# An attention and MLP layer on one core: the rotary halves share partitions, and the scores run as pairs of 64-row matmuls later in the stage

## The reference

```python
xn = layernorm(x)
q, k, v, g = xn @ Wq.T, xn @ Wk.T, xn @ Wv.T, xn @ Wg.T      # 16 heads of 128
q, k = rope(q), rope(k)            # [x1*cos - x2*sin, x2*cos + x1*sin]
s = clip(xn @ Ws1.T @ Ws2.T + bs2, -32, 32)                  # 64 slots a head
es, enz = exp(s), exp(-cumlogsumexp(s))                      # along the tokens
A = tril(q @ k.T * DK ** -0.5)
qv = softmax(enz * (A @ es))
o = tril((qv * enz) @ es.T) @ v
attn = (rmsnorm(o) * g_norm_weight * silu(g)) @ Wo.T
ffn = (gelu(xn @ Wgate.T) * (xn @ Wup.T)) @ Wdown.T          # 4-bit codes with scales
out = x + attn + ffn
```

## Time and profile before

| what | value |
|---|---|
| median of 3 runs | 1186.56 us (1185.05 to 3839.03) |
| profiled execution, its own time | 1186.13 us |
| its span, first to last instruction | 1184.4 us |
| PE, busy share | 94% |
| DVE, busy share | 80% |
| ACT, busy share | 54% |
| POOL, busy share | 35% |
| granted PE clock, mean | 0.986 |

### The profile page before, as it was taken

One profiled execution on the slowest core, in us unless ns is written; L12 is line 12 of the kernel. 1 busy time (PEld: TensorE's weight loads), 2 busy tenths in 40 slices (PEclk: granted clock), 3 DMA queues, 4 the chain that ended last, 5 costly groups with the idle time before them and its releaser, 6 DMA issues.

```text
span 1184.4 us, 20879 instructions
## 1 busy us (share of the span) xinstructions
PE 1114.7 (94%) x6872; PEld 941.6 (79%) x6872; DVE 943.1 (80%) x1808; ACT 642.1 (54%) x1748; POOL 419.6 (35%) x306
## 2 busy tenths in 40 slices
PE   6789999999999998999989999899998999999995
PEld 5568888888788887888878888788887888788884
DVE  6888887888868887888877888778886888877763
ACT  5355564655645565555655556464563565655451
POOL 5233242433513335232443324343251433523231
PEclk9899999999999999999999999999999999999998
DMA  4001000100001000010000100001000100000001
GB/s 157 1 1 74 1 1 1 52 22 1 1 2 73 1 1 2 1 73 1 1 3 1 74 1 1 3 16 59 1 1 2 73 1 1 1 2 19 1 19 36
DMA packets 9117, 23.19 MB, mean 20 GB/s; under 512 B 816, under 2 KB 5808, under 8 KB 7984
## 3 DMA queue, kind: packets, MB, share of 16 engines
q1 hardware_dynamic: 9008, 21.76, 5.0%
HBM read 19.66 MB, written 2.10 MB: 18 GB/s over the span
## 4 chain that ended last, share of the span: by engine, by line
PE 71%; issue 8%; DVE 6%; ACT 6%; POOL 3%; POOLq 0%; DVEq 0%; ACTq 0%
PE bank L203 17%; PE bank L205 16%; PE bank L204 16%; PE bank L292 5%; ACT xs L568 3%; PE bank L305 3%; PE bank L349 2%; DVE xs L860 2%; POOL qkT L1087 2%; PE bank L294 2%; DVE Wt L740 2%; ACT xs L567 2%; PE bank L282 1%; PE bank L338 1%; PE bank L341 1%
## 5 line engine op out<-in xcount | busy, mean ns | idle before, releaser
L1096 POOL TENSOR_TENSOR inter_lo<-ffb,inter_hi 128x512 fp32r<-128x512 f32 x64 | 83.3, 1323 | 433.2 <-ACT inter_hi L617 433.2
L1087 POOL TENSOR_TENSOR qkT<-ra,xs 128x512 f32<-128x512 f32 x128 | 163.5, 1277 | 95.1 <-DVE xs L860 67.6
L586 ACT ACTIVATE sm<-bank,mx 128x64 f32<-128x64 f32 x256 | 76.3, 325 | 168.5 <-DVE mx L816 168.5
L857 DVE TENSOR_TENSOR ra<-bank,rope 128x512 f32<-128x512 f32 x128 | 88.0, 687 | 55.1 <-ACT xs L568 54.9
L805 DVE RECIPROCAL enzT<-enzT 128x256 f32<-128x256 f32 x64 | 111.6, 1744 | 0.0
L860 DVE TENSOR_TENSOR xs<-xs,rope 128x512 f32<-128x512 f32 x128 | 109.0, 852 | 0.0
L203 PE MATMUL bank<-xh,wqk_hi 128*128 128x512 f32 x256 | 107.4, 420 | 0.0
L203 PE MATMUL bank<-xh,wgu_hi 128*128 128x512 f32 x256 | 106.9, 418 | 0.0
L591 ACT ACTIVATE At<-bank 128x128 f32<-128x128 f32 x128 | 35.4, 276 | 132.0 <-DVE At L740 132.0
L205 PE MATMUL bank<-xh,wgu_lo 128*128 128x512 f32 x256 | 101.6, 397 | 0.0
L203 PE MATMUL bank<-wvg_hi,xh 128*128 128x512 f32 x256 | 101.4, 396 | 0.0
(11 more groups left out here) (137 smaller groups left out, 3211.5 us busy)
## 6 DMA issues: line engine op xcount, KB each, us to landing
raw<-in_w_qkvg SPq DMA_DIRECT2D x8, 1024.0 KB, 4.9
scaled<-in_w_scaled SPq DMA_DIRECT2D x8, 640.0 KB, 7.7
packed<-in_w_packed SPq DMA_DIRECT2D x8, 384.0 KB, 5.4
acc<-in_x SPq DMA_DIRECT2D x4, 512.0 KB, 8.6
out<-acc SPq DMA_DIRECT2D x4, 512.0 KB, 3.0
ws_raw<-in_w_slot SPq DMA_DIRECT2D x8, 48.0 KB, 1.8
rope<-in_rope_tab SPq DMA_DIRECT2D x1, 256.0 KB, 7.0
osq<-in_w_slot SPq DMA_DIRECT2D x1, 128.0 KB, 3.3
```

The source lines that it names most:

```text
L857: dve.tensor_tensor(two(ra[i % 2][:, :]), two(pj[i][:, :]), cos, ALU.mult).then_inc(cos_done, 1)
L1087: pool.tensor_tensor(qkT[:, i, :], ra[i % 2][:, :], xs[i % 2][:, :], ALU.add).then_inc(roped, 1)
L1096: pool.tensor_tensor(inter[1][e][:, :], ffb[e][:, :], inter[0][e][:, :].bitcast(F32), ALU.subtract).then_inc(inter_lo, 1)
```

## The change

Five edits belong together. The weights are laid out on the host so that a projection tile holds the same half of both heads: tile 0 has the first half of q of head 0 on partitions 0 to 63 and of head 1 on 64 to 127, tile 1 their second halves, tiles 2 and 3 the same for k. With this both operands of the rotation stand on the same partitions, `swap_halves` is gone from ACT, DVE makes eight products a stage straight from PSUM, and POOL subtracts or adds. The scores contract over 64 rows twice, as pairs of the two heads. The `sc` banks no longer alternate from stage to stage. On PE the scores move behind MLP tiles 1 and 2, `slot_weights` of sequence 1 moves ahead of q and k projection 3, the `es` transposes move ahead of `slot_weights` of sequence 0, and v and gate projection 2 moves behind `slot_rows`.

```diff
@@ PE
-                pe.wait_ge(cos_done, 4 * st + i + 1)
+                pe.wait_ge(rope_mul, 8 * st + 4 * (i // 2) + 3 + i % 2)
...
-            def scores(st, bp, i, hp):
-                h, b = i // 2, i % 2
-                if b == 0:
-                    pe.wait_ge(roped, 4 * st + 2 * h + 2)
-                dst = sc_bank(bp, "A", i)
+            def scores(st, b):
                 t0 = b * T
-                pe.matmul(dst[:, 0:T], qkT[:, 2 * h + 1, t0:t0 + P], qkT[:, 2 * h, t0:t0 + T],
-                          start=True, stop=True)
-                pe.matmul(dst[:, T:T + P], qkT[:, 2 * h + 1, t0 + P:t0 + T], qkT[:, 2 * h, t0 + P:t0 + T],
-                          start=True, stop=True).then_inc(A_full, 1)
+                pair = [(sc[h], slice(h * HALF, (h + 1) * HALF)) for h in range(2)]
+                for half in range(2):
+                    for dst, g in pair:
+                        pe.matmul(dst[:, 0:T], qkT[g, 2 + half, t0:t0 + P], qkT[g, half, t0:t0 + T],
+                                  start=half == 0, stop=half == 1)
+                for half in range(2):
+                    for dst, g in pair:
+                        mm = pe.matmul(dst[:, T:T + P], qkT[g, 2 + half, t0 + P:t0 + T],
+                                       qkT[g, half, t0 + P:t0 + T], start=half == 0, stop=half == 1)
+                mm.then_inc(A_full, 2)
...
-                for i in (0, 1):
...
-                    scores(st, bp, i, hp)
                 mlp_up(st, bp, hp, 0)
                 mlp_up(st, bp, hp, 1)
-                for i in (2, 3):
-                    pe.wait_ge(A_off, 4 * st + i - 1)
-                    scores(st, bp, i, hp)
+                pe.wait_ge(roped, 4 * st + 4)
+                if first:
+                    pe.wait_ge(J_ready, 1)
+                    pe.wait_ge(clip_done, 1)
+                else:
+                    pe.wait_ge(W_off, 4 * st)
+                scores(st, 0)
                 mlp_up(st, bp, hp, 2)
+                pe.wait_ge(A_off, 4 * st + 2)
+                scores(st, 1)
                 mlp_up(st, bp, hp, 3)
@@ ACT
-                if not last:
-                    swap_halves(st + 1, 0)
-                    swap_halves(st + 1, 1)
+                if not last:
+                    copy_J(st + 1, rg[1][:, :])
@@ DVE
-            def rope_cos(n, i):
-                dve.wait_ge(swapped, 4 * n + i + 1)
-                wait(dve, roped, 4 * n + i - 1)
-                dve.tensor_tensor(two(ra[i % 2][:, :]), two(pj[i][:, :]), cos, ALU.mult).then_inc(cos_done, 1)
-
-            def rope_sin(n, i):
-                dve.tensor_tensor(two(xs[i % 2][:, :]), two(xs[i % 2][:, :]), sin, ALU.mult).then_inc(sin_done, 1)
+            def rope_first(n, t):
+                dve.wait_ge(qk_full, 4 * n + 2 * t + 2)
+                wait(dve, roped, 4 * n + 2 * t - 1)
+                dve.tensor_tensor(two(by_cos[:, 0, :]), two(pj[2 * t][:, :]), cos, ALU.mult).then_inc(rope_mul, 1)
+                dve.tensor_tensor(two(by_sin[:, 0, :]), two(pj[2 * t + 1][:, :]), sin, ALU.mult).then_inc(rope_mul, 1)
+
+            def rope_second(n, t):
+                wait(dve, roped, 4 * n + 2 * t)
+                dve.tensor_tensor(two(by_sin[:, 1, :]), two(pj[2 * t][:, :]), sin, ALU.mult).then_inc(rope_mul, 1)
+                dve.tensor_tensor(two(by_cos[:, 1, :]), two(pj[2 * t + 1][:, :]), cos, ALU.mult).then_inc(rope_mul, 1)
...
+                gate_gelu(st, 0)
+                hidden(st, 0)
+                diagonal(*a_args, 0, mask_a, (ok_full, st))
+                diagonal(*a_args, 1, mask_a, (ok_full, st))
@@ POOL
-                    for i in range(4):
-                        rotate(st + 1, i)
-                        if i == 1 and bp == 3 and more:
-                            split_lo(hp + 1, W_GU)
+                    rotate(st + 1, 0)
+                    if bp == 3 and more:
+                        split_lo(hp + 1, W_GU)
+                    rotate(st + 1, 1)
@@ on the host
-    qk = np.stack([q, k], axis=4).reshape(HP, P, KT, 512)
+    q, k = (w.reshape(HP, P, KT, 2, 2, HALF).swapaxes(3, 4) for w in (q, k))
+    qk = np.stack([q, k], axis=3).reshape(HP, P, KT, 512)
```

More of the change, by code:

```diff
@@ L94, in build @@
         qkT = sb("qkT", [P, 4, TOK])
-        xs = [sb(f"xs{i}", [P, TOK]) for i in range(2)]
-        ra = [sb(f"ra{i}", [P, TOK]) for i in range(2)]
+        by_cos = sb("by_cos", [P, 2, TOK])
+        by_sin = sb("by_sin", [P, 2, TOK])
         vS = [sb(f"vS{i}", [P, NT, 256]) for i in range(2)]
@@ L302, in slot_reads @@
                     c = b * T
-                    halves = [(rg[0][h * M:(h + 1) * M, :], At[2 * h + b], slice(h * M, (h + 1) * M)) for h in range(2)]
+                    halves = [(rg[0][h * M:(h + 1) * M, :], At[2 * b + h], slice(h * M, (h + 1) * M)) for h in range(2)]
                     for dst, a, m in halves:
@@ L321, in slot_weights @@
                 t0 = b * T
-                pair = [(sc_bank(bp, "W", 2 * b + h), slice(h * M, (h + 1) * M)) for h in range(2)]
+                pair = [(sc[h], slice(h * M, (h + 1) * M)) for h in range(2)]
                 for dst, g in pair:
@@ L460, in stage @@
                     outputs(st, 0, php, None)
-                if not last:
+                else:
                     project_vg(st + 1, nbp, nhp, 2, True)
-                slot_rows(st, bp)
+                slot_rows(st)
+                if not last and not first:
+                    project_vg(st + 1, nbp, nhp, 2, True)
                 if not first:
@@ L498, in stage @@
                 values(st, bp, 0)
-                if not last:
-                    pe.wait_ge(es_ready, st + 2)
-                    pe.wait_ge(W_off, 4 * st + 3)
-                    slot_transpose(sc_bank(bp, "E", 0), esT[nbp % 2])
                 if first:
@@ L505, in stage @@
                     pe.wait_ge(h1_lo, 4)
+                elif not last:
+                    pe.wait_ge(J_ready, st + 2)
                 values(st, bp, 1)
@@ L693, in stage @@
                     prepare_out(hp + 1)
-                softmax_exp(st, bp)
+                softmax_exp(st)
                 if not last:
@@ L710, in stage @@
                     x_hi(3)
-                if not last:
-                    swap_halves(st + 1, 2)
-                    swap_halves(st + 1, 3)
                 off_diagonal(*w_args, 2, 1.0)
@@ L718, in stage @@
                 square_o(st, 0)
-                if not last:
-                    copy_J(st + 1, sc_bank(bp, "E", 0)[:, :])
                 square_o(st, 1)
@@ L965, in stage @@
                     gate_o(npar, 0)
+                    gate_o(npar, 1)
+                gate_arg(st, 1)
                 diagonal(*a_args, 2, mask_a, (ok_full, st))
-                if not first:
-                    gate_o(npar, 1)
-                gate_gelu(st, 0)
                 diagonal(*a_args, 3, mask_a, (ok_full, st))
-                hidden(st, 0)
                 if first:
                     normalise(2)
-                gate_arg(st, 1)
+                gate_gelu(st, 1)
+                hidden(st, 1)
                 if not first:
```

125 lines of the change are left out of this document (49 added, 76 removed).

## The result

The changed kernel took 1201.7 us (median of 4 runs, 1200.5 to 1202.6) against 1186.1 us before: a ratio of 1.0134, with a 95% interval of 1.0114 to 1.0154. That is 1.3% slower: within 2% of no change, but the interval leaves no doubt of the sign. One of the four runs before took 3839 us and is left out of the ratio. The forecast was 1204 us, in a range of 1183 to 1218. So the total came out as said. Whether its terms did is another matter, and two of them did not come from where the prediction had them.

A forecast was written before the change was run, and what follows sets the result against it. PE was taken as the bound, busy 33.89 of 34.29 us in a stage. From 1186.1 us, the terms -24.8 + 23.9 + 3.4 + 17.5 + 1.3 - 3 = +18.3 gave 1204 us, range 1183 to 1218.

The forecast's parts named there:

- groups of half-array scores: Scores as 64-row pairs on PE: entering and leaving two groups costs 0.77 us a stage, +23.9 us over 31 stages.
- head waits: PE waits at the second scores: 0.2 us in 17 stages, +3.4; 1.25 us in 14 stages behind a decode, +17.5.
- waits at the transposes: PE's waits ahead of the `es` transposes go, since these now stand behind two q and k projections: -24.8 us.
- moved at no cost: `slot_weights` 1 ahead of projection 3 and `slot_rows` behind output projection are covered on PE; no time added.
- The first stage: First stage: loses its wait for the first rotation, but the second scores wait some 3 us; +1.3, between -1 and +3.
- The clock: Fewer stretches of PE at half clock after long gaps, one or two at 1.9 us each: -3, between 0 and -7.
- The back edges: PE's five waits ahead of the scores at the loop's turns, 9.7 us with nobody to wait for, stay.
- rival 2: `slot_weights` 1 waits too, its margin of 0.25 us being thin: 0.5 us in 31 stages, 1220 us; chance 0.12.
- Rival 1: Head of the stage in time, DVE's chain ending 1.1 us earlier, second scores never wait: -20.9, 1183.5 us; chance 0.17.
- Rival 3: The two heads' half-array score matmuls don't run side by side: 2.6 us a stage over 32, 1287 us; chance 0.04.
- rival 4: The way in and out of half-array score groups is hidden: -23.9, 1180.5 us; chance 0.04 alone, 0.03 with rival 1.

The follow-up runs named there:

- a_split_reads: The changed kernel with `slot_reads`, one group of half-array matmuls, cut in two with two output projections between the parts: 1214.8 us, ratio 1.0232.
- a_best: The changed kernel with the edits of a_decode and a_diag_first, and POOL's low gate and up weights ahead of rotation 0 in the opening: 1183.5 us, ratio 0.9962.
- b_es_ahead: The kernel before with only the `es` transposes moved ahead of `slot_weights` of sequence 0 and the `sc` banks fixed: 1183.7 us, ratio 0.9963.
- b_split_last: The kernel before with only POOL's low part of the MLP weights moved behind the last rotation at the end of `bp` 3: 1176.3 us, ratio 0.9901.
- a_diag_first: The changed kernel with DVE's two diagonals of the first scores put ahead of `hidden` of MLP tile 1: 1192.9 us, ratio 1.0047.
- a_decode: The changed kernel with decode parts 1 and 3 moved from the ends of `bp` 1 and 2 to within `bp` 2: 1193.2 us, ratio 1.0058.
- a_in_turn: The changed kernel with each head's two 64-row score matmuls one behind the other, then the other head's: 1209.8 us in a single run.
- b_unrolled: The kernel before with only the loop over head pairs written out, so no engine has a back edge: 1181.7 us, ratio 0.9942.
- b_split_last_unrolled: The kernel before with POOL's low MLP weights behind the last rotation and the loop over head pairs written out: 1170.4 us, ratio 0.9860.
- b_split_third: The kernel before with the loop written out and POOL's low MLP weights behind the third rotation instead of the second: 1161.3 us, ratio 0.9780.

## Why the prediction was right, and where it was not

**The groups of half-array scores (+23.9 forecast).** Right in kind, a little high in size. The row read for a group was 0.385 to 0.40 us; the changed kernel's own scores show 0.40 by the same reading. By whole stages the net of all moves on PE is 0.32 a group (34.52 against 33.88 us for two), so +20 over 31 stages, and the stages of a_split_reads show 0.33 for another sort of group. How the 0.08 between the readings divides between the group and PE's other moves is not settled. Without this term a_best would be some 20 us faster than it is; with it and the head waits the change loses.

**The waits at the transposes (-24.8).** The waits went, as forecast, but the step "They now stand behind two q and k projections, where `es` has long been ready" is not enough for it. Of the seven long waits none went by that move (b_es_ahead: 3 to 4 us in all); in the kernel before they came from POOL's instruction (b_split_last), by way of the sine product and the diagonals behind it. The prediction had found the collision in the earlier trace rows and wrote of it only to ask if it could come back. It did not ask what the move alone would do when `values`, further on in PE's order, needs `W_off` of the same pair. What covers `values` is the edit that the prediction put under "moved at no cost": `slot_weights` of sequence 1 ahead of projection 3 has its diagonals done before POOL's instruction starts, and the copies ready 0.3 us before `values`. So the size of the term came out right with half of its cause unnamed. By the order of the rows, products with both inputs in SBUF would not have brought these waits back; what they would have delayed is the rotation, MLP tile 0 and the first scores. No run has that order with the old products, or the new products with the old order, so the two are not told apart by an experiment.

**The first stage (+1.3).** This step failed: the opening took 4.0 us more, 4.4 with the stage behind it, outside the stated -1 to +3. The scores' move leaves MLP tile 0 as the first work of the stage, and its low weights are made by POOL behind rotation 0. The changed kernel's opening in order of time:

```profile
33.53 2.35 POOL L1041 TENSOR_TENSOR wgu_lo<-raw,wgu_hi 128x1024 fp32r<-128x1024 f32 x1
...
35.94 0.80 PE L199 MATMUL bank<-xh,wgu_hi 128*128 128x512 f32 x1 [5.36 <-POOL wgu_lo L1041]
36.53 0.63 PE L200 MATMUL bank<-xl,wgu_hi 128*128 128x512 f32 x1
36.96 0.63 PE L201 MATMUL bank<-xh,wgu_lo 128*128 128x512 f32 x1
```

PE waits 5.36 us, and then runs its matmuls 0.43 us apart instead of 0.23, at half the granted clock. The prediction wrote that the stage "loses its wait for the first rotation (mlp tiles cover it)", and did not follow the covering tiles to their own inputs. In a_best, with POOL's low part made earlier and two other edits, the first softmax transposes come 5.0 us earlier, 2.0 of them by the diagonals' move as a_diag_first shows.

**The head waits (+3.4 and +17.5).** Right, both in place and nearly in size. 0.24 instead of 0.2 us where no decode is in the way; 1.05 instead of 1.25 us where one is. The working had the decode delay the second scores by 1.05 more than elsewhere, and it is 0.81.

**The clock (-3).** Too small for the turns. The turn of the earlier trace rows had a mean clock of 0.96, and the same one after has 1.00; of the seven turns none has a slow stretch where four had, in one trace of each. At 1.9 us each that is 7 to 8 us. The prediction also read the 38.43 us as a stage with both sorts of gap, while of the long ones that stretch holds the back edge's alone; the 1.9 us that it took from it (35.76 less 33.89 of PE busy) are not touched by that. The gain was partly paid back: the opening and the end have more such stretches than before, which is why the mean clock hardly moved (0.986 to 0.987). That these errors, 4 us too little gain at the turns, 3 us too little cost at the opening and 1.5 at the end, cancelled was luck.

**The back edges ("stay").** Nearly: 7.7 us instead of 9.7 for the five.

**`slot_weights` of sequence 1, `slot_rows`, the rotary sums: moved at no cost.** Right. None of them waits between the first stage and the last ones, so rival 2 did not come. Rival 1 (the head in time) did not come by itself; a_decode and a_diag_first gave 8.6 and 8.8 us of it, where it was priced at 20.9, and in a_best the `bp` 1 to 3 stages gave 16.1 together. Rival 3 fell with the changed kernel's own rows, 1.51 us for a group where the columns of heads in turn alone would have made it 2.6, and rival 4 with the same rows and a_split_reads.

So the total of 1204 was right within 2.3 us: by the groups and the head waits, whose sizes held within about a fifth, by a term for the transposes whose size held for a reason that was only half named, and by luck, since the errors of the opening and the clock had opposite signs.

## What to carry to other kernels

A wait has a place and a cause, and only the second is worth an edit: before a waiting instruction is moved, ask which other instruction needs the same semaphore next, and look at what held the last producer. Here that was one operation of an engine nobody waits for, running beside a DVE operation with both inputs in SBUF, and moving it by two places gave 1.0%; by one place, with the loop written out (0.6% by itself), 2.2%. The changed kernel with the loop written out was not run. A layout that cuts a full contraction into two halves is paid on the bounding engine, 0.3 to 0.4 us for each group here, so it has to remove more than that from the path, and whether copies saved on an engine at 54% give anything was not tested here. Work that is moved to the front of a stage brings its own inputs with it, above all in the first stage.

## What the runs showed that was not expected

- The order in which the two heads' matmuls stand within a half-array group hardly matters: 1.62 against 1.51 us for a group (a_in_turn, one run).
- The loop's back edge costs PE 0.8 to 2.7 us of idle time, with nobody to wait for, in each kernel that has the loop, and nothing in the three that have it written out. Written out, the program reaches its first softmax transposes 2.2 us later (65.6 instead of 63.4 us; the cause is open), so over five back edges it pays.
- The stretches at half clock came at turns with gaps, but not in all of them: b_es_ahead has a turn of 38.68 us with the granted clock at 1.00 and some 4.5 us of gaps, and others of 40.3 to 40.6. b_unrolled, with one gap of 2.0 us, had one in six of seven turns. What brings them on in the one case and not in the other was not settled. b_split_last_unrolled, whose longest gap between 79 and 1143 us of the span was 1.7 us, and b_split_third, whose longest between 79 and 1131 us was 1.0 us, had none there.
- The mean clock varies from run to run, and the time with it: the kernel before took 1184 to 1192 us, at 0.990 and 0.977, and b_unrolled varies by 13 us. b_split_third stays within 3.
